# Second mixture-of-experts layer: one table of sums that starts as x, scatters ordered at expert borders, all weights resident, and an attention prologue written out further

## What is computed

```
x = x + tanh(g_xattn[0]) * window_attention(layernorm(x), ctx, ctx)       # 16 heads of 16, window of 64 to each side
x = x + tanh(g_ffn[0])   * moe0(layernorm(x))                             # 32 experts, 8 for a token, and a shared one
x = x + tanh(g_xattn[1]) * cross_attention(layernorm(x), ctx)             # 4 sequences of 512
x = x + tanh(g_ffn[1])   * moe1(layernorm(x))                             # 8 experts, 2 for a token, and a shared one

def moe1(x):
    scores = softmax(x @ gate_w.T); idx = top_k(scores + gate_bias, 2)
    for e in range(8):
        gate_e = sum(where(idx == e, scores[idx], 0))
        y = y + gate_e * ((silu(x @ w1[e].T) * (x @ w3[e].T)) @ w2[e].T)  # inner width 256
    return y + (silu(x @ sw1.T) * (x @ sw3.T)) @ sw2.T                    # shared, width 512
```

## Time and profile before

| what | value |
|---|---|
| median of three runs | 1072.34 us |
| profiled execution | 1076.61 us, of which the span from first to last instruction is 1074.8 us |
| PE busy | 917.3 us, 85% of the span |
| DVE busy | 701.5 us, 65% |
| POOL busy | 538.5 us, 50% |
| ACT busy | 440.9 us, 41% |
| moved by DMA | 131.50 MB, mean 122 GB/s |
| granted TensorE clock, mean | 0.932 of full speed |

### The profile page before, as it was taken

How to read it: one execution, slowest core, us unless ns; L and a number is a source line. 1 busy time by engine, 2 the same in 40 slices (tenths; PEclk the granted TensorE clock), 3 DMA queues, 4 the chain that set the end, 5 groups by cost and what they waited for, 6 DMA issues and landing times.

```text
span 1074.8 us, 20627 instructions
## 1 busy us (share of the span) xinstructions
PE 917.3 (85%) x5524; PEld 714.3 (66%) x5525; DVE 701.5 (65%) x1983; ACT 440.9 (41%) x1031; POOL 538.5 (50%) x582
## 2 busy tenths in 40 slices
PE   3458888888667999999999977989999998998893
PEld 2357777777545888888887644756666564786672
DVE  6669999998596875555554397775856156443334
ACT  4558888893143444444343402031323223232220
POOL 7246665554003777555551777777400001787651
PEclk9779999998667999999999989989999997999997
DMA  8860000002601787776777794343200020467648
GB/s 244 222 134 2 1 0 0 0 2 85 220 1 45 224 237 226 208 237 206 219 175 137 207 389 129 111 139 108 78 1 20 1 79 18 82 114 136 132 76 249
DMA packets 79209, 131.50 MB, mean 122 GB/s; under 512 B 12496, under 2 KB 56016, under 8 KB 78992
## 3 DMA queue, kind: packets, MB, share of 16 engines
q0 software_dynamic: 21264, 48.02, 20.6%
q1 hardware_dynamic: 36224, 61.53, 18.9%
q10 hardware_dynamic: 21632, 20.85, 5.6%
HBM read 80.62 MB, written 40.83 MB: 113 GB/s over the span
## 4 chain that ended last, share of the span: by engine, by line
PE 56%; DVE 23%; DMA 9%; issue 6%; SPq 2%; ACT 2%; POOL 2%; DVEq 0%; ACTq 0%; POOLq 0%
PE bank L923 17%; PE bank L938 9%; PE bank L1661 5%; DVE ptl L627 4%; PE bank L912 4%; DMA sw<-in_w 3%; DVE nmax L619 3%; PE bank L1559 2%; PE bank L931 2%; DVE hot_hi L1378 2%; PE bank L433 2%; PE bank L1596 2%; PE bank L1719 2%; PE bank L1621 2%; SPq L2026 1%
## 5 line engine op out<-in xcount | busy, mean ns | idle before, releaser
L1201 POOL DMA_INDIRECT xg<-token_rows,gather_idx x198 | 191.4, 967 | 200.2 <-DVE gather_idx L1409 68.5
L923 PE MATMUL bank<-sw,xgt 128*128 x948 | 244.9, 381 | 0.4 <-issue 0.4
L923 PEld LDWEIGHTS bank<-sw,xgt 128*128 128x128 f32 x948 | 165.4, 191 | 15.3 <-issue 0.8
L1236 POOL DMA_INDIRECT yg<-slot_rows,slot_of x128 | 134.2, 1048 | 60.4 <-issue 33.5
L1017 ACT ACTIVATE ssil<-bank 128x128 f32<-128x128 f32 x237 | 65.8, 278 | 206.5 <-PE bank L923 206.5
L938 PE MATMUL bank<-sw,sht 128*128 x474 | 145.4, 389 | 0.1
L1118 DVE COPY xgt<-bank 128x256 f32<-128x256 f32 x198 | 83.8, 424 | 83.9 <-PE bank L912 68.1
L1131 DVE COPY sht<-bank 128x128 f32<-128x128 f32 x237 | 69.1, 291 | 106.4 <-PE bank L931 105.9
L555 ACT ACTIVATE prob<-bank,nmax 128x256 f32<-128x256 f32 x256 | 111.8, 512 | 8.0 <-DVE nmax L619 8.0
L433 PE MATMUL bank<-consts,prob 128*128 128x128 f32 x512 | 82.6, 285 | 37.0 <-DVE ptl L627 34.8
L619 DVE TENSOR_REDUCE nmax<-bank 128x2 f32<-128x512 f32 x128 | 87.6, 685 | 16.5 <-PE bank L420 16.0
(11 more groups left out here) (228 smaller groups left out, 1623.7 us busy)
## 6 DMA issues: line engine op xcount, KB each, us to landing
slot_rows<-ysb ACTq DMA_DIRECT2D x79, 256.0 KB, 3.3
sw<-in_w SPq DMA_DIRECT2D x48, 384.0 KB, 3.9
kst<-khl SPq DMA_DIRECT2D x32, 224.0 KB, 5.2
token_sums<-zeros SPq DMA_DIRECT2D x2, 2176.0 KB, 25.2
token_rows<-xn SPq DMA_DIRECT2D x8, 512.0 KB, 4.1
sums<-token_sums SPq DMA_DIRECT2D x8, 512.0 KB, 7.8
slot_rows<-zeros SPq DMA_DIRECT2D x1, 3968.0 KB, 15.4
xg<-token_rows,gather_idx POOLq DMA_INDIRECT x198, 3.6
```

What stands on the lines that cost most here:

```text
L923: mm = pe.matmul(bank[2 + k % 2][:, 0:2 * FF], xgt[:, i % 3, c * P:(c + 1) * P], w[:, :, c, :], start=(c == 0), stop=(c == CH - 1))
L1201: nc.gpsimd.indirect_dma_start(xg[:, (first + i) % XG_RING, 0:ROW[L]], None, rows[L], bass.IndirectOffsetOnAxis(gather_idx[:, i:i + 1], 0) ...
L1236: nc.gpsimd.indirect_dma_start(yg[:, t % Y_TILES, j, :], None, ybuf[L], bass.IndirectOffsetOnAxis(slot_of[:, t, j:j + 1], 0)).then_inc(s_y ...
```

## The change

Seven edits. None changes what is multiplied.

1. *Attention of layer 0.* Six tiles are written out where there were two (`STATIC`), and the loop runs over eight. PE waits for piece 1 of the keys ahead of tile 2, and for piece 2 only in the loop, ahead of tile 9. `EARLY` moves four of the eight parts to later steps, the split of key piece 2 from step 8 to 18; two of the layernorm statistics move from steps 10 and 12 to 20 and 28.
2. *Tokens are numbered anew.* Token number p x 16 + t instead of t x 128 + p. A partition's rows then lie together in memory, and tokens of a tile that follow each other are 16 rows (16 KiB) apart.
3. *One table of sums.* It is not cleared. SP stores x into it, batch by batch (`x_to_sums`). Only 256 spare rows are zeroed, and that is done in the attention of layer 0, as is the zeroing of `slot_rows`.
4. *Ordered scatters.* A block whose expert differs from the one before it waits until that one has landed. SP waits for it and counts up a semaphore for POOL (`scattered_by_turns`).
5. *Copy out.* When the blocks in use have landed SP copies the table to the output by two transfers from memory to memory (`copied_out`). Loads of sums, additions on DVE and stores of x are gone.
6. *Weights of layer 1.* All 16 halves have a place (`w1all`). It takes the space of `yg0`, `wsh0` and `sw`, so four halves are loaded early in the attention of layer 1, and twelve once the last row of layer 0 has been added. PE waits for both loads once.
7. *Routing of layer 1.* The one-hot rows of 16 tiles have their own places, written by five pairs of instructions; the wait for the ring is gone. `shared_down` for batch 3 moves from the end to ahead of the expert blocks, and its addition on DVE behind the second `slots_copied`.

```diff
-            for t in (0, 1):
+            for t in range(STATIC):
+                if t == 2:
+                    pe.wait_ge(s_kst[1], 256)
+                    pe.wait_ge(s_vd, 2 * len(VGROUPS) - 2)
+                    pe.wait_ge(s_band, BATCH)
                 for k in range(PAIRS):
-                    step(t, k, t, False)
-            for piece in (1, 2):
-                pe.wait_ge(s_kst[piece], 256)
+                    step(t, k, t % 2, False)
             pe.wait_ge(s_vd, 2 * len(VGROUPS))
-            pe.wait_ge(s_band, BATCH)
-            with pe.Fori(0, (TILES - 4) // 4) as i:
+            with pe.Fori(0, (TILES - 2 - STATIC) // 4) as i:
                 for j in range(4):
+                    if STATIC + j == KEYS2_TILE:
+                        pe.wait_ge(s_kst[2], 256)
...
-        EARLY = {0: ("v", 0, 1), 2: ("v", 1, 0), 4: ("v", 1, 1), 5: ("v", 2, 0), 7: ("v", 2, 1), 8: ("k", 2, 0),
-                 10: ("v", 3, 0), 12: ("v", 3, 1)}
+        EARLY = {0: ("v", 0, 1), 2: ("v", 1, 0), 4: ("v", 1, 1), 8: ("v", 2, 0), 11: ("v", 2, 1), 18: ("k", 2, 0),
+                 24: ("v", 3, 0), 32: ("v", 3, 1)}
+        STATS = {3: 1, 20: 2, 28: 3}
...
+                pe.wait_ge(s_w1[0], 16)
+                pe.wait_ge(s_w1[1], 16)
...
-                    if L == 1:
-                        pe.wait_ge(s_sw, loads[i])
...
             slots_copied(1)
+            if L == 1:
+                shared_added(dve, m, BATCH - 1)
+                experts_bounded(dve)
...
             if i >= 2:
                 pool.wait_ge(s_scat[i % 2], 16 * (i // 2))
+            if i in (1, 2):
+                pool.wait_ge(s_scat[(i - 1) % 2], 16)
+            elif i >= 3:
+                pool.wait_ge(s_turn, i - 2)
             nc.gpsimd.indirect_dma_start(
-                total[i % 2], bass.IndirectOffsetOnAxis(scatter_idx[:, i:i + 1], 0), ysb[:, i // 2 % Y_RING, i % 2, :],
+                total, bass.IndirectOffsetOnAxis(scatter_idx[:, i:i + 1], 0), ysb[:, i // 2 % Y_RING, i % 2, :],
                 None, compute_op=ALU.add).then_inc(s_scat[i % 2], 16)
...
+        def experts1_loaded(sp, part):
+            first, last = ((2 * E1 - W_RING, 2 * E1), (0, 2 * E1 - W_RING))[part]
+            if part:
+                sp.wait_ge(moe[0].y, BATCH)
+                sp.wait_ge(s_yadd, TOP0 * TILES)
+            sp.dma_start(w1all[:, first:last, :],
+                         w1_in[SH1 + first:SH1 + last].rearrange("u p c -> p u c")).then_inc(s_w1[part], 16)
...
+        def x_to_sums(sp, b):
+            ts = slice(TPB * b, TPB * b + TPB)
+            sp.wait_ge(moe[1].acc, moe[1].n["acc"] + TPB * b + TPB)
+            sp.dma_start(total[0:TOKENS, :].rearrange("(p t) c -> p t c", p=P)[:, ts, :], x[:, ts, :]).then_inc(s_summed, 16)
+
+        def scattered_by_turns(sp):
+            for i in range(3, BLOCKS[1]):
+                before = sp.value_load(turn[0:1, i - 1:i], min_val=16, max_val=16 * ((i - 1) // 2 + 1))
+                sp.wait_ge(s_scat[(i - 1) % 2], before)
+                sp.sem_inc(s_turn, 1)
+
+        def copied_out(sp):
+            last = [sp.value_load(ended_n[0:1, r:r + 1], min_val=16, max_val=16 * len(range(r, BLOCKS[1], 2)))
+                    for r in range(2)]
+            for r in range(2):
+                sp.wait_ge(s_scat[r], last[r])
+                sp.sem_inc(s_used, 1)
+            sp.wait_ge(s_used, 2)
+            half = P // 2
+            by_part = total[0:TOKENS, :].rearrange("(p t) c -> p t c", p=P)
+            for h in range(2):
+                sp.dma_start(out[h * half:(h + 1) * half, :, :], by_part[h * half:(h + 1) * half]).then_inc(s_out, 16)
...
-            kept_busy(pe, bank[7], 8)
+            shared_down(pe, m, b)
+            kept_busy(pe, bank[0], 2)
...
             shared_hidden(b, 2)
-            hots(range(TILES))
+            hots(((0, 4), (4, 8)))
+            shared_hidden(b, 3)
+            hots(((8, 12), (12, 14), (14, 16)))
             weights()
             indices()
-            shared_hidden(b, 3)
...
-            for i in range(2):
-                sp.wait_ge(s_scat[i], 16 * len(range(i, BLOCKS[1], 2)))
-            for b in range(BATCH):
-                for i in range(2):
-                    by_tile = total[i][0:TOKENS, :].rearrange("(t p) c -> p t c", p=P)
-                    sp.dma_start(sums[:, b, i], by_tile[:, TPB * b:TPB * b + TPB, :]).then_inc(s_sum[b], 16)
-            for b in range(BATCH):
-                sp.wait_ge(s_yadd, TOP0 * TILES + 2 * b + 2)
-                sp.dma_start(out[:, b * TPB:(b + 1) * TPB, :], x[:, b * TPB:(b + 1) * TPB, :]).then_inc(s_out, 16)
```

More of the change, by code:

```diff
@@ L94, in gated_xattn_moe_kernel @@
         ybuf = [nc.dram_tensor(f"slot_rows{L}", (BLOCKS[L] * SLOTS, DIM), F32).ap() for L in range(2)]
-        total = [nc.dram_tensor(f"token_sums{i}", (TOKENS + P, DIM), F32).ap() for i in range(2)]
+        total = nc.dram_tensor("token_sums", (TOKENS + 2 * P, DIM), F32).ap()
         a0 = ExitStack()
@@ L141, in gated_xattn_moe_kernel @@
         spare = sb("spare", [P, BLOCKS[1]], F32)
-        spare_id = sb("spare_id", [P, 1], F32)
-        zeros = sb("zeros", [P, DIM], F32)
-        gate_of = sb("gate_of", [P, TILES, 8], F32)
-        fin = ExitStack()
-        sums = sb("sums", [P, BATCH, 2, TPB, DIM], F32, fin)
-        fin.close()
+        spare_id = sb("spare_id", [P, 2 * PAIRED[1]], F32)
+        turn_base = sb("turn_base", [1, 2 * PAIRED[1]], F32)
+        boundary = sb("boundary", [1, BLOCKS[1] - 1], F32)
+        turn = sb("turn", [1, BLOCKS[1] - 1], I32)
+        ended = sb("ended", [1, 2], U32)
+        ended_n = sb("ended_n", [1, 2], I32)
+        gate_of = sb("gate_of", [P, TILES, 8], F32)
+        w1scope = ExitStack()
+        w1all = sb("w1all", [P, 2 * E1, WCOLS], F32, w1scope)
+        w1scope.close()
+        wsh0 = sb("wsh0", [P, WCOLS], F32)
+        beside = sb("beside", [P, DIM], F32)
         yg0 = sb("yg0", [P, Y_TILES, TOP0, DIM], F32)
+        sw = sb("sw", [P, W_RING, WCOLS], F32)
         landed = sb("landed", [1, Y_RING], U32)
@@ L563, in step @@
                         k_hi(g)
-            for t in (0, 1):
+            for t in range(STATIC):
                 for k in range(PAIRS):
-                    step(t, k, t, False)
-            with act.Fori(0, (TILES - 4) // 4) as i:
+                    step(t, k, t % 2, False)
+            with act.Fori(0, (TILES - 2 - STATIC) // 4) as i:
                 for j in range(4):
                     for k in range(PAIRS):
-                        step(4 * i + 2 + j, k, j % 2, False)
+                        step(4 * i + STATIC + j, k, j % 2, False)
             for t in (TILES - 2, TILES - 1):
@@ L636, in step @@
                         k_lo(g)
-            for t in (0, 1):
+            for t in range(STATIC):
                 for k in range(PAIRS):
-                    step(t, k, t, False)
+                    step(t, k, t % 2, False)
             dve.wait_ge(s_lnp[0], 2 * BATCH)
-            with dve.Fori(0, (TILES - 4) // 4) as i:
+            with dve.Fori(0, (TILES - 2 - STATIC) // 4) as i:
                 for j in range(4):
                     for k in range(PAIRS):
-                        step(4 * i + 2 + j, k, j % 2, False)
+                        step(4 * i + STATIC + j, k, j % 2, False)
             for t in (TILES - 2, TILES - 1):
@@ L718, in attention_pool @@
             pool.wait_ge(s_tg, 1)
-            tile(0, 0)
-            tile(1, 1)
-            with pool.Fori(0, (TILES - 4) // 4) as i:
+            for t in range(STATIC):
+                tile(t, t % 2)
+                if t == 2:
+                    for g in range(4):
+                        pool.wait_ge(s_kst0[g], 64)
+                    nc.gpsimd.memset(zeros, 0.0).then_inc(s_zero, 1)
+            with pool.Fori(0, (TILES - 2 - STATIC) // 4) as i:
                 for j in range(4):
-                    tile(4 * i + 2 + j, j % 2)
+                    tile(4 * i + STATIC + j, j % 2)
             for t in (TILES - 2, TILES - 1):
@@ L904, in sparse_tensor @@
             first, blocks, halves = FIRST[L], BLOCKS[L], 1 + L
+            wt, last = (sw, w1all)[L], (W_RING - 1, 2 * E1 - 2)[L]
             slot = {}
@@ L945, in sparse_tensor @@
                 pe.wait_ge(m.acc, m.n["acc"] + 12)
[L946 removed]
+                pe.wait_ge(s_w1[0], 16)
+                pe.wait_ge(s_w1[1], 16)
             def block_numbers(i):
[L949 to L951 removed]
+                slot[i] = pe.value_load(wslot[0:1, i:i + 1], min_val=0, max_val=last)
             block_numbers(0)
@@ L957, in sparse_tensor @@
                 i = k // halves
-                if k % halves == 0:
-                    if L == 1:
-                        pe.wait_ge(s_sw, loads[i])
-                    if i + 2 < blocks:
-                        slots_transposed(i + 2)
+                if k % halves == 0 and i + 2 < blocks:
+                    slots_transposed(i + 2)
                 gate_up(k)
@@ L968, in sparse_tensor @@
                 if k >= 2:
```

(8 more changed lines are left out.)

178 lines of the change are left out of this document (102 added, 76 removed).

## The result

The changed kernel takes 1046.71 us (median of four runs, 1045.04 to 1049.40) where the kernel before, run beside it, takes 1072.74 (1069.45 to 1074.91): 0.9762 of the time, 95% interval 0.9729 to 0.9796, or 22 to 29 us less. The forecast was 1038, with a range of 1026 to 1054. The profiled execution took 1045.04 us, of which the span is 1043.2.

What follows compares the result with a forecast made beforehand. DVE was taken to bound layer 0's attention, PE the experts, a chain the end. Terms -14 + 4.4 - 7.7 - 16.5 = -33.8 us took the profiled 1076.6 to 1042.8, the median to 1038.5; forecast 1038, range 1026 to 1054.

Steps and rivals of the forecast that it cites:

- signs of being wrong: PE idle on layer 0 gathers, DMA share near 1, scatters over 5 us, layer 1 gather waits, copy over 12 us.
- What bounds the kernel: DVE paces layer 0's attention, PE its experts; layer 1's experts keep PE busy but for short stops; the end is a chain.
- the five stops for weights: Experts of layer 1: PE waits 5.3 us for weights in five stops, 11.6 us apart.
- Attention, -14: Attention of layer 0: DVE's idle time at two stops goes, its work only moves; 14 us less.
- the stop only moves: Rival, chance 0.11: ACT is also full, tiles 2 to 4 stretch or piece 1 lands later; attention gives 6, kernel 1046.
- Start, +4.4: Start of layer 1's experts: more PE passes in shared_down and DVE additions delay the first block by 4.4 us.
- Weights, -7.7: Experts of layer 1: PE's weight waits, 5.3 us, and the 2.4 us right behind them go; 7.7 us less.
- Scatters, the step that failed: Layer 1's ordered scatters and copy out: seven borders cost POOL 1.0 us each without reaching PE; with the copy, -16.5 us.
- 2.5 us of lag: Experts of layer 1: POOL's remaining delay at block 35, the last in use, after making up 1.3 us a block.
- borders cost more: Rival, chance 0.12: landings of 5.5 us make a border 2.7 us, seven 19, and the kernel 1051.
- End: After block 35's scatter: landing 3.8 us, SP's answer, copy 8.5; PE's unused blocks and their scatters over by 1051.
- The other rivals: Rows far apart slow layer 0's gathers, chance 0.05, up to 1131 us; the gains cancel, chance 0.03, 1072.

Runs made afterwards that it cites:

- old attention: The changed kernel with edit 1 undone (two tiles written out, both key pieces waited for ahead of the loop): 1062.1 us, 0.9905 of the kernel before.
- the run without the last product: The changed kernel without the shared expert's last product and addition for batch 3, eight unread products in place: 1044.8 us, 0.9744 of the kernel before.
- two tables: The changed kernel with even and odd blocks scattered to separate tables, no border waits, odd blocks missing from the output: 1035.8 us, 0.9661 of the kernel before.
- numbering alone: The kernel before with only the tokens numbered p x 16 + t: 1071.5 us for 1073.1, ratio 0.9978.
- LAG 13: The changed kernel with thirteen gathers ahead of the first scatter, where it had eight: 1045.0 us, 0.9731 of the kernel before.
- used blocks only: The changed kernel without the scatters of the three unused blocks: 1043.0 us, 0.9723 of the kernel before.

## Why the prediction held, and where it failed

The measured 1046.7 us lie inside the range of 1026 to 1054 and 8.7 above the forecast. Two of the forecast's signs of being wrong came: PE waits for gathers in layer 1, and scatters land in over 5 us, these only beside the copy.

*What bounds the kernel.* Right for the attention, layer 0's experts and the five stops for weights.

*Attention, -14.* The mechanism was right, the size too large: 10.8 by the two profiles, 10.5 by the old attention in the changed kernel, 12.0 by the means of all profiled executions. The term took the freed time at the 96% of the steady loop. The stretch is not the steady loop: DVE reaches 83% in it, since it waits 4.7 us for PE, mostly in windows of a lowered clock, and 2.4 us for ACT's halves of the splits. The forecast had watched ACT for this ("the stop only moves"), not PE. That the clock is what holds DVE there was not tried.

*Start, +4.4.* Right to 0.1 us by the first scatter (PE's first gate-up came 3.3 us later for the 3 forecast), and the run without the last product shows that it is that edit. What the forecast didn't say is that half of it would be lost in POOL's backlog anyway.

*Weights, -7.7.* PE has no such wait left, and the profile after shows it. The forecast missed that without the reading of `needed` and the wait on it a block is also 0.15 us shorter, 5 us over 36 blocks. Together PE could have had 13 us; the stage got 1.0, because POOL became the bound.

*Scatters, the step that failed.* "At each of seven borders ... 1.0 us more" and "they lead PE by six blocks, 20 us, so seven borders do not reach PE. From block 31 on there are no gathers and POOL makes up 1.3 us a block; I leave 2.5 us of lag at block 35." POOL's waits at borders sum to 13.5 us, and the first three scatters cost 3.3. The step set POOL's 3.2 us against 3.3 for PE, the pace of before, where the weights and the second read went; against 3.04 POOL is slower in every block that has a gather, as the 3.19 with two tables shows. It does not catch up by block 35, and in the last blocks there is no gather to fill a border, so POOL idles 3.0 us there. The rival "borders cost more" named the price but the wrong cause: landings at the borders are 3.8 us as forecast. In place of the 2.5 us of lag the order costs 13 us by the two tables.

*End.* Landing 3.8, SP's answer and a copy of 8.0 for 8.5 came as said: without unused scatters and their drain in the way it is 12.5 us from block 35's scatter on, and the forecast had 12.9. The step "PE's three unused blocks and their scatters are over by 1051" left out what POOL does behind its last scatter. That drain was in the trace of before, under 15 us of other work, and was not looked for; it cost 4.5 us by its trace, and the unused scatters beside the copy, with landings of 8 to 9 us, the rest of 6.9. The Trainium skill, "VectorE: DVE Perf Modes", "The DRAIN you can't avoid", tells of the runtime's opening and closing drains, about 12 ns each on all five engines. Those at the end of this kernel's own block of programs are other ones: in the changed kernel SP's has 7 ns, DVE's 330, ACT's 486, PE's 628 and POOL's 12,779, so the figure can't be carried over to them.

*The other rivals.* The gathers were not slowed by rows 16 KiB apart: 3.4 us each in the page of after, and numbering alone changes nothing. The Trainium skill, "DMA: Bandwidth & Descriptors", "Latency and other measured facts", measured its loss at pitches of 512 KiB and more; the 16 KiB of this kernel show none.

What stays open: how much of DVE's idle time from 36 to 75 us a full clock would give back, and what the 0.06 us a block are that the second read doesn't explain.

## What to carry to other kernels

When a change takes waits from one engine, compare its new pace, not its old one, with the engine that feeds it, and count that engine's own chain (here scatter, landing, next scatter) over the whole stage: a queue's lead hides a fixed delay, not a slower rate. A wait that names the starved engine (PE for gathers) may only show it: LAG 13 took all of it away and the kernel gained 1.7 us, less than the intervals can tell. Before shortening the last chain of a kernel, look at what every engine still does at its end, since work that was covered sets the end next.

## What the runs showed of the hardware

- POOL's closing drain ends 4.5 to 5.5 us after its last indirect transfer has landed (5.5 in the kernel before, 4.5 in the changed one, 5.2 with used blocks only), so it is longer where that landing is slow: 9.3 us with a landing of 3.7, 12.8 with one of 8.0.
- Two accumulating scatters that must follow each other start 4.6 us apart, though the second's data is ready: 3.8 to land and 0.8 until POOL begins.
- Memory to memory, 2.1 MB in two transfers land in 6.6 to 8.1 us (6.7 in the one run with no scatter beside them). A scatter beside that copy lands in 8.0 to 9.0 us in the changed kernel, for 3.8.
- A number that PE reads for a block, without waiting on it, costs 0.09 us a block of 3.04, by one profiled execution of each kernel.
